# Attention scores of a head pair: two bursts of 64-row products become one, and score and projection banks are shared

## The chip, the cores and the metric

One Trainium2 chip, one of its cores. The number that counts is the device time of one launch in microseconds (us). The kernel before takes 2736.12 us, the median of three runs (2734.57 to 2736.74).

## The reference

For 32 sequences (batch index b) of 256 rows of width 256: a cross attention with 16 heads of width 64 over 512 keys (256 rows of a side tensor and 256 rows of a context tensor, each with weights of its own), a residual, then a small quantised layer, and a second residual.

```python
q = layernorm(x) @ Wq.T + bq                          # 16 heads of 64
k = concat(side @ Wk.T + bk, ctx @ Wgk.T + bgk)       # 512 keys
v = concat(side @ Wv.T + bv, ctx @ Wgv.T + bgv)
att = q @ k.T / 8;  att[..., :256] = where(mask, -inf, att[..., :256])
x = x + softmax(att) @ v @ Wo.T + bo
x = x + fp8_gemm(layernorm(x), kernel) + ffn_bias
```

## The kernel before

Everything is written in five instruction streams, one for each engine, in an order written out by hand for one batch. The streams run a first batch, a hardware loop over the next 30 and a last batch. The engines meet only through semaphores; no scheduler moves anything.

Per batch the stream of TensorE (PE) holds 89 calls of four kinds.

- `scores(c, h, t)`: the scores of one tile of 128 query rows for the head pair h, h+1. A head is 64 wide, so a product uses 64 of the array's 128 rows: the two heads of a pair lie in the two halves of the partitions, and their products start together. Numbers are split into a high and a low part, so three products are summed: k_hi by q_hi, k_hi by q_lo, k_lo by q_hi. A call is thus a burst of 3 steps of 2 products, 512 columns each. There are 16 such calls a batch: 8 pairs by 2 tiles. They write the PSUM tensor `ps_scores`, two banks, one for each head of the pair.
- `chunk(c, kind, n)`: a projection into one bank of `ps_misc` (two banks, taken in turn). Kinds k0, k1, v0, v1 and q are keys, values and queries of head group n (12 products of 128 rows and 256 columns each); wo0 and wo1 are the output projection of the batch before (16 matmul records each); xq, ff and zt are short.
- `transposes(c, h, k)`: four 128 by 128 transposes of the normalised probabilities of head h, into `ps_pt` (two banks).
- `outputs(c, h)`: probabilities times values, 8 products, into `ps_o` (two banks).

The other engines follow. VectorE (DVE) `mins` (L1144) adds the mask to a bank of scores, writes `probs` and takes the row minimum; ScalarE (ACT) `exps` (L875) takes exponentials; DVE `recip`, then GpSimd (POOL) `norm` (L477) scales; after the transposes ACT `pt_his` (L882) and DVE `pt_los` (L1155) split the result into high and low parts. `o_los` on ACT (L889) and `o_adds` on DVE (L1163) empty `ps_o`. Projections are emptied by `copy_keys` on ACT (L852), `split_his` on ACT (L840) with `split_los` on DVE (L1050), or `copy_values` on DVE (L1075); POOL splits keys and values once more.

What sets the order around the change: before a `scores` call PE waits on `min_done` until the minima of the two heads of the tile before have been taken (the one buffer of scores is empty). Before a `chunk` it waits on `misc_free` of that chunk's bank. `probs` is a ring of four heads: minima of head h wait for the transposes of the heads up to h-4, and for h+1 up to h-3.

Of the kernel before, what the change touches and what calls it, by code (L numbers as in the profile page):

```python
# [33 lines left out]
P = 128  # L34
# [49 lines left out]
MISC_BANKS = 2  # L84
KV_RING = 4
BANK = {chunk: i % MISC_BANKS for i, chunk in enumerate(CHUNKS)}
# [11 lines left out]
class Batch:  # L98
# [20 lines left out]
    def before(self, chunk, kinds, bank=None):  # L119
        return self.earlier(kinds, bank) + counted(self.chunks[:self.chunks.index(chunk)], kinds, bank)  # L120

# [23 lines left out]
def xattn_ffn_kernel(nc, x, side_t, ctx_t, mask, wq_t, bq, wk_t, bk, wgk_t, bgk, wv_t, bv, wgv_t, bgv,  # L145
                     wo_t, bo, ffn_w, s_in, s_k, ffn_bias, out):
    with ExitStack() as ctx:
# [89 lines left out]
        misc_full = [sem(f"misc_full{i}") for i in range(MISC_BANKS)]  # L237
        misc_free = [sem(f"misc_free{i}") for i in range(MISC_BANKS)]
# [12 lines left out]
        kvhi_done = sem("kvhi_done")  # L251
# [151 lines left out]
        def _(pool):  # L403
# [23 lines left out]
            def split_rows(c, part):  # L427
# [3 lines left out]
                if not (isinstance(c.b, int) and c.b < 0):  # L431
                    chunk = (("v0", 3), ("v1", 3))[part]
                    pool.wait_ge(misc_full[BANK[chunk]], c.through(chunk))
# [5 lines left out]
                nc.gpsimd.tensor_scalar(kv_hi[:, :, keys], raw, 1.0, 0.0, ALU.mult, ALU.add).then_inc(kvhi_done, 1)  # L439
                pool.wait_ge(kvhi_done, 2 * (n - 1) + part + 1)  # L440
# [19 lines left out]
            def kv_hi_of(c, kind, n):  # L460
                if (kind, n) in c.chunks:
                    src, hi, _ = kv_parts(kind, n)
                    wait_apart(pool, "pool", misc_free[BANK[kind, n]], c.through((kind, n)))
                    nc.gpsimd.tensor_scalar(hi, src, 1.0, 0.0, ALU.mult, ALU.add).then_inc(kv_hi_part, 1)  # L464
# [20 lines left out]
            def add_ffn_bias(c):  # L485
                if not c.first:
                    pool.wait_ge(misc_free[BANK["ff_prev", 0]], c.through(("ff_prev", 0)))
# [20 lines left out]
            def batch(c):  # L508
# [6 lines left out]
                kv_hi_of(c, "k1", 1)  # L515
                norm(c, 3, 0)
                norm(c, 3, 1)
                kv_lo_of(c, "k1", 1)
                rstd_of_y(c)
                copy_x(c)  # L520
                norm(c, 4, 0)
                norm(c, 4, 1)
                kv_hi_of(c, "v0", 1)
                norm(c, 5, 0)
                norm(c, 5, 1)
                scale_quant_in(c)
                kv_lo_of(c, "v0", 1)
# [5 lines left out]
                norm(c, 6, 0)  # L533
                norm(c, 6, 1)
                kv_lo_of(c, "v0", 2)
                norm(c, 7, 0)
                norm(c, 7, 1)
                kv_hi_of(c, "k1", 2)
                kv_lo_of(c, "k1", 2)
                kv_hi_of(c, "v1", 2)  # L540
                kv_lo_of(c, "v1", 2)
                norm(c, 8, 0)
                norm(c, 8, 1)
                norm(c, 9, 0)
                kv_hi_of(c, "k0", 3)
                norm(c, 9, 1)
                rstd_of_x(c)
# [3 lines left out]
                split_rows(c, 0)  # L551
                norm(c, 10, 0)
                norm(c, 10, 1)
                kv_hi_of(c, "v0", 3)
                norm(c, 11, 0)
                norm(c, 11, 1)
                split_rows(c, 1)
                kv_lo_of(c, "v0", 3)
                kv_hi_of(c, "v1", 3)
                norm(c, 12, 0)  # L560
                norm(c, 12, 1)
                norm(c, 13, 0)
                kv_lo_of(c, "v1", 3)
                kv_hi_of(c, "k0", 0)
                norm(c, 13, 1)
                kv_lo_of(c, "k0", 0)
                add_ffn_bias(c)
                norm(c, 14, 0)
                norm(c, 14, 1)
                kv_hi_of(c, "v0", 0)  # L570
                kv_lo_of(c, "v0", 0)
                finish(c)
                norm(c, 15, 0)
                norm(c, 15, 1)
                kv_hi_of(c, "k1", 0)
                kv_lo_of(c, "k1", 0)
                kv_hi_of(c, "v1", 0)
                norm(c, 16, 0)
                norm(c, 16, 1)
                kv_lo_of(c, "v1", 0)  # L580

# [12 lines left out]
        def _(pe):  # L594
# [11 lines left out]
            def chunk(c, kind, n):  # L606
                if (kind, n) not in c.chunks:
                    return
                if kind == "q" and n == 0:
                    pe.wait_ge(misc_free[BANK["zt_next", 0]], c.through(("zt_next", 0)))  # L610
# [8 lines left out]
                if kind == "ff_prev":  # L619
                    pe.wait_ge(misc_free[BANK["xq_prev", 0]], c.through(("xq_prev", 0)))  # L620
                bank = BANK[kind, n]
                if some(c.fills_before((kind, n))):
                    pe.wait_ge(misc_free[bank], c.fills_before((kind, n)))
                run_chunk(kind, n, bank).then_inc(misc_full[bank], 1)

            def run_chunk(kind, n, bank):

                halves = [ps_misc[:, bank, j * S:(j + 1) * S] for j in range(2)]
# [37 lines left out]
            def scores(c, h, t):  # L666
# [5 lines left out]
                if t == 0:  # L672
                    for ready in needed:
                        through = c.through if h >= H or n > 0 else c.through_last
                        if ready[0] == "q":
                            pe.wait_ge(misc_free[BANK[ready]], through(ready))
# [47 lines left out]
            scores(c, H, 0)  # L724
            scores(c, H, 1)
            pe.wait_ge(wo_loaded, 16)

            def batch(c):
                chunk(c, "k0", 1)
                scores(c, 2, 0)  # L730
                outputs(c, -1)
                transposes(c, 0, 0)
                transposes(c, 0, 1)
                scores(c, 2, 1)
                chunk(c, "q", 1)
                transposes(c, 1, 0)
                transposes(c, 1, 1)
                outputs(c, 0)
                chunk(c, "wo0_prev", 0)
                chunk(c, "k1", 1)  # L740
                transposes(c, 2, 0)
                transposes(c, 2, 1)
                scores(c, 4, 0)
                chunk(c, "wo1_prev", 0)
                scores(c, 4, 1)
                chunk(c, "q", 2)
                transposes(c, 3, 0)
                outputs(c, 1)
                scores(c, 6, 0)
                transposes(c, 3, 1)  # L750
                chunk(c, "v0", 1)
                chunk(c, "k0", 2)
# [630 lines left out]
```

## Time and profile before

| | |
|---|---|
| median of three runs | 2736.12 us |
| the profiled execution | 2734.6 us |
| span of its trace | 2732.8 us |
| PE busy | 2677.5 us, 98% |
| DVE busy | 2163.6 us, 79% |
| POOL busy | 2048.8 us, 75% |
| ACT busy | 1859.6 us, 68% |
| granted TensorE clock, mean | 0.995 |

The span lies between the first and the last instruction of the profiled execution; the execution's own time is 1.8 us longer. A start in the timeline is the moment a group of instructions begins; matmuls overlap, so the cost of a PE instruction is read from the distance between two starts, not from its duration. In the chain of work each piece lasts until the next one of the chain begins.

### The profile page before, as it was taken

The numbers are of one execution on the slowest core, as the hardware profiler recorded it, in microseconds if no ns is written. First come the engines' busy times: TensorE is split into PE (matmuls) and PEld (weight loads), VectorE is DVE, ScalarE is ACT, GpSimd is POOL, SyncE is SP. The second block draws the span as 40 slices with busy tenths as digits, with TensorE's granted clock in tenths as the row PEclk, the third lists the DMA queues.
The fourth block names the chain that finished last, engine by engine and source line by source line (L and its number), as shares of the span: only waits on it lengthen the run. The fifth ranks groups of instructions, "written<-read, shape, count | busy, mean of one in ns | idle before, by whom it ended". The sixth has DMA issues, their size and how long they took to land.

```text
span 2732.8 us, 66539 instructions
## 1 busy us (share of the span) xinstructions
PE 2677.5 (98%) x20352; PEld 2349.6 (86%) x20352; DVE 2163.6 (79%) x5329; ACT 1859.6 (68%) x4454; POOL 2048.8 (75%) x2503
## 2 busy tenths in 40 slices
PE   5999999999999999999999999999999999999996
PEld 4888888888888888888888888888888888888885
DVE  5888777888778887778877788887788877788875
ACT  4766667766667666677666676666776666776664
POOL 4787777877777877777877778777788777787774
PEclk9999999999999999999999999999999999999998
DMA  3000000001000000000000000000000100000100
GB/s 144 24 24 24 27 27 23 27 19 31 23 27 27 27 19 27 27 23 27 19 31 23 27 27 27 19 27 27 26 24 19 31 27 24 26 27 19 31 16 8
DMA packets 57246, 75.18 MB, mean 28 GB/s; under 512 B 4992, under 2 KB 39296, under 8 KB 57216
## 3 DMA queue, kind: packets, MB, share of 16 engines
q1 hardware_dynamic: 57216, 74.81, 9.0%
q8 instruction: 15, 0.25, 0.0%
q14 instruction: 15, 0.12, 0.0%
HBM read 66.40 MB, written 8.39 MB: 27 GB/s over the span
## 4 chain that ended last, share of the span: by engine, by line
PE 80%; ACT 7%; issue 6%; DVE 5%; DMA 0%; SPq 0%; POOL 0%; DVEq 0%; ACTq 0%; POOLq 0%
PE ps_misc L603 28%; PE ps_scores L685 15%; PE ps_o L712 15%; PE ps_pt L697 13%; PE ps_misc L653 8%; ACT probs L875 3%; DVE probs L1144 2%; ACT pt_hi L882 2%; DVE pt_lo L1155 2%; ACT kv_out L852 1%; DVE o_t L1163 1%; PE ps_misc L662 1%; PE ps_misc L632 0%; DMA probs<-wv_t_dram 0%; ACT q_hi L840 0%
## 5 line engine op out<-in xcount | busy, mean ns | idle before, releaser
L477 POOL TENSOR_SCALAR probs<-probs,recips 128x512 f32<-128x512 f32 x1024 | 729.7, 723 | 330.2 <-DVE recips L1151 324.2
L875 ACT ACTIVATE probs<-probs,neg_max 128x512 f32<-128x512 f32 x1024 | 739.7, 725 | 214.8 <-DVE neg_max L1144 205.4
L1144 DVE CUSTOM_DVE_ANT_1 probs<-ps_scores,mask_sb 128x512 f32<-128x512 f32 x960 | 636.2, 685 | 217.9 <-PE ps_scores L685 177.6
L882 ACT CAST pt_hi<-ps_pt 128x512 fp32r<-128x512 f32 x1024 | 565.6, 589 | 306.7 <-PE ps_pt L697 300.0
L1155 DVE TENSOR_TENSOR pt_lo<-ps_pt,pt_hi 128x512 fp32r<-128x512 f32 x1024 | 675.6, 683 | 108.1 <-ACT pt_hi L882 107.0
L697 PE MATMUL ps_pt<-ident,probs 128*128 128x128 f32 x4096 | 554.2, 274 | 6.1 <-POOL probs L477 3.7
L712 PE MATMUL ps_o<-pt_hi,v_hl 128*128 128x256 f32 x2048 | 548.6, 302 | 3.0 <-DVE pt_lo L1155 3.0
L712 PE MATMUL ps_o<-pt_lo,v_hl 128*128 128x256 f32 x2048 | 508.1, 282 | 0.0
L697 PEld LDWEIGHTS ps_pt<-ident,probs 128*128 128x128 f32 x4096 | 457.3, 141 | 46.8 <-issue 35.5
L712 PEld LDWEIGHTS ps_o<-pt_hi,v_hl 128*128 128x128 f32 x2048 | 387.0, 189 | 62.0 <-issue 58.0
L712 PEld LDWEIGHTS ps_o<-pt_lo,v_hl 128*128 128x128 f32 x2048 | 389.3, 190 | 0.0
L470 POOL TENSOR_TENSOR v_hl<-kv_out,v_hl 128x512 fp32r<-128x512 f32 x256 | 346.7, 1354 | 8.1
L470 POOL TENSOR_TENSOR k_lo<-kv_out,k_hi 128x512 fp32r<-128x512 f32 x256 | 331.5, 1295 | 13.4
L889 ACT COPY o_lo<-ps_o 64x256 f32<-64x256 f32 x512 | 189.6, 370 | 181.2 <-DVE o_t L1163 167.0
L464 POOL TENSOR_SCALAR k_hi<-kv_out 128x512 fp32r<-128x512 f32 x256 | 166.2, 649 | 169.3 <-ACT kv_out L852 169.3
L685 PE MATMUL ps_scores<-k_hi,q_hi 64*128 64x512 f32 x1024 | 256.2, 497 | 6.2 <-DVE neg_max L1144 3.2
L852 ACT ACTIVATE kv_out<-ps_misc,qk_bias 128x256 f32<-128x256 f32 x512 | 215.4, 475 | 57.7 <-PE ps_misc L603 55.3
L464 POOL TENSOR_SCALAR v_hl<-kv_out 128x512 fp32r<-128x512 f32 x256 | 175.5, 686 | 93.4 <-DVE kv_out L1075 93.4
L653 PE MATMUL ps_misc<-wo_sb,o_t 128*128 128x256 f32 x1024 | 237.7, 386 | 1.5 <-DVE o_t L1163 0.9
L653 PEld LDWEIGHTS ps_misc<-wo_sb,o_t 128*128 128x128 f32 x1024 | 191.6, 192 | 37.4 <-issue 12.2
L1163 DVE TENSOR_TENSOR o_t<-ps_o,o_lo 64x256 f32<-64x256 f32 x480 | 198.5, 414 | 27.2 <-ACT o_lo L889 20.2
L685 PE MATMUL ps_scores<-k_hi,q_lo 64*128 64x512 f32 x1024 | 203.3, 393 | 0.0
(105 smaller groups left out, 5846.1 us busy)
## 6 DMA issues: line engine op xcount, KB each, us to landing
mask_sb<-mask_dram SPq DMA_DIRECT2D x128, 256.0 KB, 3.1
x_sb<-x_dram SPq DMA_DIRECT2D x32, 256.0 KB, 2.7
side_raw<-side_t_dram SPq DMA_DIRECT2D x32, 256.0 KB, 3.8
scr_b<-ctx_t_dram SPq DMA_DIRECT2D x32, 256.0 KB, 2.7
out_dram<-y SPq DMA_DIRECT2D x32, 256.0 KB, 2.1
probs<-wq_t_dram SPq DMA_DIRECT2D x1, 1024.0 KB, 5.0
o_t<-wk_t_dram SPq DMA_DIRECT2D x1, 1024.0 KB, 7.3
wo_sb<-wgk_t_dram SPq DMA_DIRECT2D x1, 1024.0 KB, 9.3
```

Source lines behind the costliest of these rows:

```text
L464: nc.gpsimd.tensor_scalar(hi, src, 1.0, 0.0, ALU.mult, ALU.add).then_inc(kv_hi_part, 1)
L470: nc.gpsimd.tensor_tensor(lo, src, hi.bitcast(F32), ALU.subtract).then_inc(kv_ready, 1)
L477: nc.gpsimd.tensor_scalar(p, p, recips[:, h % RING, t:t + 1], 1.0, ALU.mult, ALU.mult).then_inc(norm_done, 1)
L603: last = mm(dst, a(t), c(t), start=(n == 1), stop=(n == 3 * DT))
L653: last = mm(dst, o_t[:, p, tile], wo_sb[:, p, :], start=(p == 0), stop=(p == H // 2 - 1))
L685: last = mm(ps_scores[:, e, :], q[own, n % 2, a, rows], k[own, n % 2, a, :], start=(i == 0), stop=(i == 2))
L697: last = nc.tensor.transpose(ps_pt[:, k, j, t * P:(t + 1) * P], probs[:, h % RING, t, kt * P:(kt + 1) * P], ident[:])
L712: last = mm(ps_o[:, h % 2, 0:S], v_hl[:, n % 2, kt, i, :], pt[:, h % 2, kt, :], start=(kt == 0 and pt is pt_hi), stop=(kt == KT - 1 and pt ...
L875: nc.scalar.activation(p, p, ACT.Exp, bias=neg_max[:, h % RING, t:t + 1], scale=-1.0, accum_out=sums[:, h % RING, t:t + 1]).then_inc(exp_d ...
L882: nc.scalar.copy(pt_hi[:, h % 2, 2 * k:2 * k + 2, :], ps_pt[:, k, :, :]).then_inc(pthi_done, 1)
L1144: V.tensor_tensor_reduce(out=p, in0=s, in1=mask_sb[:, row::MASK_ROWS - row, :], scale=MASK_STEP, scalar=SCORE_LIMIT, op0=ALU.add, op1=ALU.min,
L1155: V.tensor_tensor(pt_lo[:, h % 2, 2 * k:2 * k + 2, :], ps_pt[:, k, :, :], pt_hi[:, h % 2, 2 * k:2 * k + 2, :].bitcast(F32), ALU.subtract). ...
```

## The change

`ps_scores` and `ps_misc` become one tensor `ps_work` of four banks. `scores(c, h, 0)` writes banks 0 and 1 (one for each head of the pair), `scores(c, h, 1)` writes banks 2 and 3. The two calls now stand one behind the other for each of the eight pairs, so a burst has 6 steps of 2 products. The chunks use the same four banks, each by a table. A chunk therefore waits in addition (`after=(h, t)`) until DVE has taken the minima of the scores that lay in its bank, and a `scores` call waits until the chunks that used its two banks have been emptied (`after=` names the last of them for each bank). The work is the same, instruction for instruction; the orders of all four compute engines' streams are new. The list of chunks and the ring of `probs` stay.

```diff
+BANKS = 4
-BANK = {chunk: i % MISC_BANKS for i, chunk in enumerate(CHUNKS)}
+BANK = {
+    ("k0", 1): 0, ("q", 1): 1, ("wo0_prev", 0): 3, ("k1", 1): 2, ("wo1_prev", 0): 0,
...
-        ps_scores = psum("ps_scores", [P, 2, NK])
+        ps_work = psum("ps_work", [P, BANKS, 512])
         ps_pt = psum("ps_pt", [P, 2, 2, S])
         ps_o = psum("ps_o", [P, 2, 512])
-        ps_misc = psum("ps_misc", [P, MISC_BANKS, 512])
...
-            def chunk(c, kind, n):
+            def chunk(c, kind, n, after=None):
+
                 if (kind, n) not in c.chunks:
                     return
+                if after:
+                    h, t = after
+                    pe.wait_ge(min_done, 2 * (c.head(h) + t) + BANK[kind, n] % 2 + 1)
...
-                if some(c.head(h) + t):
-                    pe.wait_ge(min_done, 2 * (c.head(h) + t))
+                if some(c.head(h)):
+                    pe.wait_ge(min_done, 2 * (c.head(h) + t) - 2)
+                for e, chunk_before in enumerate(after):
+                    bank = 2 * t + e
+                    if some(c.so_far(chunk_before, bank)):
+                        pe.wait_ge(chunk_free[bank], c.so_far(chunk_before, bank))
...
-                        last = mm(ps_scores[:, e, :], q[own, n % 2, a, rows], k[own, n % 2, a, :],
+                        last = mm(ps_work[:, 2 * t + e, :], q[own, n % 2, a, rows], k[own, n % 2, a, :],
...
-                s = ps_scores[:, h % 2, :].rearrange("p (k s) -> p k s", s=S)
+                s = ps_work[:, 2 * t + h % 2, :].rearrange("p (k s) -> p k s", s=S)
```

The new order of PE for one batch, where the eight pairs stand (of what is left out, only the calls next to a burst are named in the prediction):

```diff
+                scores(c, 2, 0, after=(None, None))
+                scores(c, 2, 1, after=(None, None))
+                transposes(c, 0, 0)
+                transposes(c, 0, 1)
+                chunk(c, "k0", 1, after=(2, 0))
...
+                chunk(c, "k1", 1, after=(2, 1))
                 transposes(c, 2, 0)
+                scores(c, 4, 0, after=(("k0", 1), ("q", 1)))
+                scores(c, 4, 1, after=(("k1", 1), ("wo0_prev", 0)))
                 transposes(c, 2, 1)
+                chunk(c, "wo1_prev", 0, after=(4, 0))
...
+                chunk(c, "k0", 2, after=(4, 1))
+                scores(c, 6, 0, after=(("wo1_prev", 0), ("v0", 1)))
+                scores(c, 6, 1, after=(("k0", 2), ("q", 2)))
                 outputs(c, 2)
...
                 transposes(c, 5, 1)
+                scores(c, 8, 0, after=(("v1", 1), ("v0", 2)))
+                scores(c, 8, 1, after=(("k0", 2), ("k1", 2)))
                 outputs(c, 4)
...
+                chunk(c, "k1", 3, after=(8, 1))
+                scores(c, 10, 0, after=(("v1", 2), ("q", 3)))
+                scores(c, 10, 1, after=(("xq_prev", 0), ("k1", 3)))
+                outputs(c, 7)
...
                 transposes(c, 9, 1)
+                scores(c, 12, 0, after=(("v1", 2), ("q", 3)))
+                scores(c, 12, 1, after=(("v1", 3), ("v0", 3)))
+                transposes(c, 10, 0)
+                chunk(c, "zt_next", 0, after=(12, 0))
...
                 outputs(c, 10)
+                scores(c, 14, 0, after=(("zt_next", 0), ("ff_prev", 0)))
+                scores(c, 14, 1, after=(("q", 0), ("v0", 3)))
                 transposes(c, 12, 0)
...
                 outputs(c, 12)
+                scores(c, 16, 0, after=(("zt_next", 0), ("k0", 0)))
+                scores(c, 16, 1, after=(("k1", 0), ("v0", 0)))
                 transposes(c, 14, 0)
                 transposes(c, 14, 1)
+                chunk(c, "v1", 0, after=(16, 0))
```

PE before, at the second tile of the pair 6, 7: the end of the chunk v1 of group 1 (`ps_misc`), the burst (`ps_scores`), the beginning of the outputs of head 3 (`ps_o`). The burst of the first tile stands 45 rows earlier.

```order
L603 MATMUL ps_misc<-wgv_hi,kv_hi 128x256
L603 MATMUL ps_misc<-wgv_hi,kv_lo 128x256
L603 MATMUL ps_misc<-wgv_lo,kv_hi 128x256
L685 MATMUL ps_scores<-k_hi,q_hi 128x512 x2
L685 MATMUL ps_scores<-k_hi,q_lo 128x512 x2
L685 MATMUL ps_scores<-k_lo,q_hi 128x512 x2
L712 MATMUL ps_o<-pt_hi,v_hl 128x256
```

PE now, at the same pair: the end of the chunk k0 of group 2, both tiles' scores, the outputs of head 2.

```order
L614 MATMUL ps_work<-kv_hi,wgk_hi 128x256
L614 MATMUL ps_work<-kv_hi,wgk_lo 128x256
L614 MATMUL ps_work<-kv_lo,wgk_hi 128x256
L707 MATMUL ps_work<-k_hi,q_hi 128x512 x2
L707 MATMUL ps_work<-k_hi,q_lo 128x512 x2
L707 MATMUL ps_work<-k_lo,q_hi 128x512 x2
L707 MATMUL ps_work<-k_hi,q_hi 128x512 x2
L707 MATMUL ps_work<-k_hi,q_lo 128x512 x2
L707 MATMUL ps_work<-k_lo,q_hi 128x512 x2
L734 MATMUL ps_o<-pt_hi,v_hl 128x256
```

The two bursts have moved together, and the chunk ahead of them, k0 of group 2, lies in bank 2, which the second tile's scores need three steps later.

DVE before, from the minima of pair 4, 5: the minima of the first tile (each with a read of its accumulator, `neg_max`), the low parts of head 2's transposes, then the minima of the second tile with an addition between them.

```order
L1144 ISA probs,neg_max<-ps_scores,mask_sb 128x512
L1144 ISA neg_max 128x1
L1144 ISA probs,neg_max<-ps_scores,mask_sb 128x512
L1144 ISA neg_max 128x1
L1155 TENSOR_TENSOR pt_lo<-ps_pt,pt_hi 128x512 x2
L1144 ISA probs,neg_max<-ps_scores,mask_sb 128x512
L1144 ISA neg_max 128x1
L1163 TENSOR_TENSOR o_first<-ps_o,o_lo 64x256
L1144 ISA probs,neg_max<-ps_scores,mask_sb 128x512
L1144 ISA neg_max 128x1
```

DVE now, at the same pair.

```order
L1166 ISA probs,neg_max<-ps_work,mask_sb 128x512
L1166 ISA neg_max 128x1
L1166 ISA probs,neg_max<-ps_work,mask_sb 128x512
L1166 ISA neg_max 128x1
L1166 ISA probs,neg_max<-ps_work,mask_sb 128x512
L1166 ISA neg_max 128x1
L1177 TENSOR_TENSOR pt_lo<-ps_pt,pt_hi 128x512
L1166 ISA probs,neg_max<-ps_work,mask_sb 128x512
L1166 ISA neg_max 128x1
```

The four minima of a pair now follow each other almost directly; the low parts of the transposes come between or behind them.

## Rows read from the trace of the kernel before

**Rows 1.** The page: span, busy time by engine.

```profile
span 2732.8 us, 66539 instructions
PE 2677.5 (98%) x20352; PEld 2349.6 (86%) x20352; DVE 2163.6 (79%) x5329; ACT 1859.6 (68%) x4454; POOL 2048.8 (75%) x2503
```

**Rows 2.** Two stretches: length, busy PE, PEld, DVE, ACT, POOL, then PEclk, DMA.

```profile
50.00:133.00 83.00, 79.08 (x609) 69.00 (x610) 67.04 (x164) 58.29 (x142) 61.00 (x74) 1.00 0.08 24
1200.00:1283.00 83.00, 82.93 (x636) 72.88 (x635) 67.08 (x166) 57.45 (x140) 63.50 (x79) 1.00 0.09 25
```

**Rows 3.** Timeline of PE, one row in each of two batches: start, us, instruction.

```profile
1180.55 0.60 PE L632 MATMUL ps_misc<-ident,scr_a 128*128 128x128 f32 x4
1263.89 0.60 PE L632 MATMUL ps_misc<-ident,scr_a 128*128 128x128 f32 x4
```

**Rows 4.** PE's waits over the whole span: total us, times, longest us.

```profile
PE ps_misc L603 <- DVE wv_lo L1184: 8.9, 1, 8.9
PE ps_scores L685 <- DVE neg_max L1144: 3.2, 2, 1.7
```

**Rows 5.** Timeline of PE around one burst.

```profile
1206.28 0.28 PE L603 MATMUL ps_misc<-kv_lo,wgk_hi 128*128 128x256 f32 x1
1206.49 0.49 PE L685 MATMUL ps_scores<-k_hi,q_hi 64*128 64x512 f32 x2
1206.83 0.39 PE L685 MATMUL ps_scores<-k_hi,q_lo 64*128 64x512 f32 x2
1207.06 0.40 PE L685 MATMUL ps_scores<-k_lo,q_hi 64*128 64x512 f32 x2
1207.40 0.38 PE L712 MATMUL ps_o<-pt_hi,v_hl 128*128 128x256 f32 x1
1207.62 0.29 PE L712 MATMUL ps_o<-pt_lo,v_hl 128*128 128x256 f32 x1
```

**Rows 6.** The chain of work inside one batch: start, us until the next piece.

```profile
1212.90 0.95 PE ps_o L712 x8
...
1226.65 0.44 PE ps_pt L697 x4
...
1228.04 0.89 PE ps_scores L685 x6
1228.93 0.59 PE ps_pt L697 x4
1229.52 2.85 PE ps_misc L603 x24
...
1235.70 1.15 PE ps_o L712 x8
```

**Rows 7.** Timeline of PE before the loop: two bursts with nothing between.

```profile
37.81 0.40 PE L685 MATMUL ps_scores<-k_lo,q_hi 64*128 64x512 f32 x2
39.88 0.50 PE L685 MATMUL ps_scores<-k_hi,q_hi 64*128 64x512 f32 x2 [1.68 <-DVE neg_max L1144]
40.21 0.39 PE L685 MATMUL ps_scores<-k_hi,q_lo 64*128 64x512 f32 x2
```

**Rows 8.** Timeline, all engines: a chunk's last product and its emptying.

```profile
1211.74 0.28 PE L603 MATMUL ps_misc<-zt_lo,wq_hi 128*128 128x256 f32 x1
...
1212.06 0.84 ACT L840 ACTIVATE q_hi<-ps_misc,qk_bias 128x256 fp32r<-128x256 f32 x2 [0.31 <-PE ps_misc L603]
```

**Rows 9.** Timeline of ACT and of DVE: a copy of keys, one minimum.

```profile
1201.09 0.85 ACT L852 ACTIVATE kv_out<-ps_misc,qk_bias 128x256 f32<-128x256 f32 x2
...
1207.84 0.69 DVE L1144 CUSTOM_DVE_ANT_1 probs<-ps_scores,mask_sb 128x512 f32<-128x512 f32 x1 [0.25 <-issue]
1208.46 0.08 DVE L1144 DVE_READ_ACCUMULATOR2_ANT neg_max<- 128x1 f32 x1
```

**Rows 10.** DVE's longest kind of wait: total us, times, longest us.

```profile
DVE probs L1144 <- PE ps_scores L685: 177.6, 193, 2.9
```

More of the change, by code:

```diff
@@ L120, in before, with so_far @@
         return self.earlier(kinds, bank) + counted(self.chunks[:self.chunks.index(chunk)], kinds, bank)
+    def so_far(self, chunk, bank):
+        upto = CHUNKS[:CHUNKS.index(chunk) + 1] if chunk else []
+        return self.earlier(ALL_KINDS, bank) + counted([c for c in self.chunks if c in upto], ALL_KINDS, bank)
     def fills_before(self, chunk):
@@ L664, in run_chunk, with scores @@
                 return last
-            def scores(c, h, t):
+            def scores(c, h, t, after):
                 if not c.has_head(h):
@@ L758, in batch @@
                 transposes(c, 4, 1)
-                chunk(c, "v0", 2)
-                chunk(c, "k1", 2)
+                chunk(c, "v1", 1, after=(6, 0))
+                chunk(c, "v0", 2, after=(6, 0))
+                chunk(c, "k1", 2, after=(6, 1))
                 transposes(c, 5, 0)
-                scores(c, 8, 0)
                 transposes(c, 5, 1)
+                scores(c, 8, 0, after=(("v1", 1), ("v0", 2)))
+                scores(c, 8, 1, after=(("k0", 2), ("k1", 2)))
                 outputs(c, 4)
-                chunk(c, "v1", 2)
@@ L766, in batch @@
-                scores(c, 8, 1)
+                outputs(c, 5)
                 transposes(c, 6, 0)
                 transposes(c, 6, 1)
-                chunk(c, "q", 3)
-                chunk(c, "k0", 3)
+                chunk(c, "v1", 2, after=(8, 0))
+                chunk(c, "q", 3, after=(8, 0))
                 transposes(c, 7, 0)
-                outputs(c, 5)
+                chunk(c, "k0", 3, after=(8, 1))
                 transposes(c, 7, 1)
                 outputs(c, 6)
-                scores(c, 10, 0)
@@ L776, in batch @@
-                chunk(c, "xq_prev", 0)
-                chunk(c, "k1", 3)
+                chunk(c, "xq_prev", 0, after=(8, 1))
+                chunk(c, "k1", 3, after=(8, 1))
+                scores(c, 10, 0, after=(("v1", 2), ("q", 3)))
+                scores(c, 10, 1, after=(("xq_prev", 0), ("k1", 3)))
+                outputs(c, 7)
                 transposes(c, 8, 0)
                 transposes(c, 8, 1)
-                outputs(c, 7)
-                scores(c, 10, 1)
-                chunk(c, "v0", 3)
@@ L789, in batch @@
-                chunk(c, "ff_prev", 0)
-                transposes(c, 10, 0)
                 transposes(c, 10, 1)
                 outputs(c, 9)
-                scores(c, 12, 1)
-                chunk(c, "q", 0)
+                chunk(c, "ff_prev", 0, after=(12, 0))
+                chunk(c, "q", 0, after=(12, 1))
                 transposes(c, 11, 0)
                 transposes(c, 11, 1)
-                scores(c, 14, 0)
                 outputs(c, 10)
-                chunk(c, "k0", 0)
+                scores(c, 14, 0, after=(("zt_next", 0), ("ff_prev", 0)))
@@ L802, in batch @@
                 outputs(c, 11)
-                scores(c, 14, 1)
-                chunk(c, "v0", 0)
+                chunk(c, "k0", 0, after=(14, 0))
+                chunk(c, "v0", 0, after=(14, 1))
+                chunk(c, "k1", 0, after=(14, 1))
                 transposes(c, 13, 0)
@@ L834, in split_his @@
                 bank = BANK[kind, n]
-                act.wait_ge(misc_full[bank], c.through((kind, n)))
+                act.wait_ge(chunk_full[bank], c.through((kind, n)))
                 for cols, hi, _, bias in split_parts(kind, n):
                     if bias is None:
-                        last = nc.scalar.copy(hi, ps_misc[:, bank, cols])
+                        last = nc.scalar.copy(hi, ps_work[:, bank, cols])
                     else:
-                        last = nc.scalar.activation(hi, ps_misc[:, bank, cols], ACT.Identity, bias=bias)
+                        last = nc.scalar.activation(hi, ps_work[:, bank, cols], ACT.Identity, bias=bias)
                 last.then_inc(hi_done, 1)
@@ L851, in copy_keys @@
                     half = slice(j * S, (j + 1) * S)
-                    last = nc.scalar.activation(kv_out[:, KV_TURN[kind, n], half], ps_misc[:, bank, half],
+                    last = nc.scalar.activation(kv_out[:, KV_TURN[kind, n], half], ps_work[:, bank, half],
                                                 ACT.Identity, bias=qk_bias[:, 1 + j, p:p + 1])
-                last.then_inc(misc_free[bank], 1)
+                last.then_inc(chunk_free[bank], 1)
             def copy_quantised(c):
@@ L1045, in split_los @@
                 for cols, hi, lo, bias in split_parts(kind, n):
-                    src = ps_misc[:, bank, cols]
+                    src = ps_work[:, bank, cols]
                     if bias is None:
@@ L1051, in split_los @@
                                                       op0=ALU.add, op1=ALU.subtract)
-                last.then_inc(misc_free[bank], 1)
+                last.then_inc(chunk_free[bank], 1)
             def moments(which, src, bn_ready, mv_ready, n):
```

341 lines of the change are left out of this document (163 added, 178 removed), and 4 rows, old and new, of the table BANK.

## The prediction, written before the changed kernel ran

> **What bounds the kernel now.** I read the busy shares first: PE is busy for 98% of the span, DVE, the next, for 79% [rows 1]. A share can hide a stage that is bound otherwise, so the table by stretches came next. In a stretch of 83 us in the middle of the loop PE idles for 0.07 us and its clock is granted in full; the stretch that begins at 50 us shows 79.08 us of 83, so the first batch alone waits [rows 2]. The same row begins in two neighbouring batches 83.34 us apart [rows 3]; 32 batches of that are 2667 us of the 2732.8, and the rest is the start and the end. In the waits of PE the longest is 8.9 us and happens once, in the preparation of the weights; for the banks of scores PE waited twice, 3.2 us together [rows 4]. So in the loop PE runs from instruction to instruction, and time can only come from the distances between its starts, or be lost by a wait that is not there now.
>
> **What a burst costs.** Plain products of 256 columns start 0.12 us apart: two chunks in a row, 24 products, are a piece of 2.85 us in the chain of work [rows 6]. Around one burst [rows 5], from the last plain product before it (1206.28) to the second one behind it (1207.62), it is 1.34 us, of which two plain distances are 0.24: the burst costs 1.10 us. Inside it the distances are 0.34 and 0.23, and 0.34 from the third step to the first product behind. The first plain product behind takes 0.22 to the next in place of 0.12. The chain of work says the same: the piece of a burst is 0.89 us, and the outputs behind a burst are a piece of 1.15 where those behind a transpose are 0.95. Transposes behind a burst cost a little less, 0.59 for 0.44 [rows 6].
>
> Put directly behind the first, the second tile's three steps should cost the inner distance, 0.23 each: one merged burst is 1.10 + 0.69 = 1.79 us where two single ones are 2.20. That is 0.41 us for each pair. Eight pairs make 3.3 us a batch. Before, three of sixteen bursts are followed by transposes, after it is five of eight; at 0.05 us each this is 0.1 us more. Against that, starts are rounded to 0.01 us, which counts three times in each pair, and one of the sixteen bursts today is followed by the short 16-bit transposes of the quantised rows, which may lose less. I choose 0.39 us for a pair, at the lower side, **3.1 us a batch**; 3.3 stays as the upper end.
>
> The trace before has one place with two bursts and nothing between, ahead of the loop, and there PE had waited 1.68 us for minima. Behind that wait the first inner distance is 0.33 again, with no other mode in between [rows 7]. The long first step belongs to a start after a pause as well, and the seam in a merged burst costs between nothing and 0.10 us. I take nothing where its waits have been met in time: the 24 products of rows 6 are two chunks, each with a wait at its head, and their mean distance stays at 0.119.
>
> The Trainium skill (TensorEngine Tiling (Array Packing), Tiling Modes, Key Properties) says that a change of the tiling mode drains the engine, and not a change of tile in one mode. By the rule alone the seam is free and the gain 3.1 us; by rows 7, which show a long first step without a change of mode, it would be 3.1 - 8 x 0.10 = 2.3.
>
> **What the new waits cost.** Counts of instructions on DVE, ACT and POOL do not change, nor do the DMAs that SP issues or what they wait for (minima, which are all done in the same number). Four cases:
>
> *The second tile waits for a chunk directly ahead.* At two pairs a keys' chunk stands right before the burst and lies in a bank of the second tile: k0 of group 2 before pair 6 (bank 2), k1 of group 3 before pair 10 (bank 3). From the chunk's last product to the second tile's first it is 0.21 + 0.34 + 0.23 + 0.23 = 1.01 us [rows 5]. To empty a bank takes longer: a chunk's last product starts at 1211.74, ACT begins at 1212.06 and needs 0.84, so it is free at 1212.90, 1.16 us later [rows 8]; the keys' copy takes 0.85 [rows 9]. With the way back to PE I put 0.2 to 0.25 us on each, if ACT is idle at that moment, which its order allows (it holds only the copy of the transposes issued before the chunk). Two places: 0.45 us. In pair 4 the chunk k1 of group 1 is one group of four transposes (0.44 us) further off and just makes it: 1.45 against 1.16.
>
> *A chunk waits for the minima in its bank.* A minimum occupies DVE for 0.62 us and its read 0.08 [rows 9]. The near places are pairs 2, 4, 12 and 16, where the first chunk in bank 0 comes 0.4 to 0.9 us (one or two groups of transposes) behind the second tile's 0.8. So 1.2 to 1.7 us lie between the start of the gap (the first tile's last step, which runs 0.40 us on) and the chunk; the minimum with its start needs 0.40 + 0.1 + 0.7 = 1.2. It fits only if DVE stands ready. At pair 2 it does: the work in front, the addition of head 14's output, is issued before the burst. At pair 12 the low part of a transpose stands in front, at pair 16 one too, but both groups of transposes were issued before the burst. I put 0.05 us on these four together and keep 1 us each as the other end, below.
>
> *The probabilities.* Between a pair's burst and the transposes of its first head PE now has at least 6.8 us of other work (pair 16: the two groups of transposes of head 14, v1, outputs 13, transposes 15, outputs 14, then the next burst, 0.87 + 1.5 + 0.95 + 0.87 + 0.95 + 1.6). From the first minimum to the scaled row the work is four minima (2.5 us), an exponential (0.9) and two scalings on POOL (1.4), some 5.5 us with the waits. Covered with about 1.3 us to spare.
>
> *DVE as a whole.* It is busy 67.1 us of 83 now [rows 2]; of 80.7 that is 83%. Still behind PE, but its slack shrinks from 16 to 14 us a batch.
>
> **The sum.** 83.3 - 3.1 + 0.5 = 80.7 us a batch, 2.6 us less. The first batch waits for other things, so I count 31: 81 us. The profiled execution took 2734.6, which gives 2654. The median of the runs is 1.5 us above it, so 2655.
>
> **Rivals.**
>
> A, *the seam is not free*. Each of the eight seams pays the 0.10 us of rows 7 because the second tile's waits, up to three of them, stop the products of its first step from being prepared. Then the gain is 2.6 - 0.8 = 1.8 us, times 31 is 56: 2680. For it: the only two adjacent bursts in the trace. Against it: there PE stood still in between.
>
> B, *slower: DVE comes late to the banks*. Today DVE waits for scores 193 times, 177.6 us in all [rows 10]: the scores are what comes late, not DVE. After the change 4 banks fill in 1.7 us and DVE needs 2.5 us to empty them. If at the near places (pairs 2, 4, 12, 16) it first has to finish one low part that itself waits for ACT's copy (0.6 + 0.6 us), and then the second pair of minima is late for the next chunk too, PE stands for 1 us each; the other four pairs, with one 0.3 us stall each, bring it to 5.2. Less the 3.1 that is 2.1 us a batch, 65 us in all: 2801. It decides from 0.39 us lost at each pair on. Against it: in front of each of these minima, in the order of DVE, stands work whose input PE has issued before the burst. The Trainium skill (TensorEngine Tiling, PSUM Bottleneck) warns of this: tiling speeds up TensorE, not the emptying of PSUM. No row here shows a bank that is late.
>
> C, *the gain is eaten but not more*: the second tile waits at most pairs, so that bursts stay split in fact. A split burst costs 0.39 and the wait by itself 0.1 to 0.2. At half the pairs that leaves 3.1 - 4 x 0.55 = 0.9 us, 28 us in all: 2708; at all of them nothing is left.
>
> **Chances.** My forecast 0.66, A 0.14, C 0.09 (of it 0.02 within 0.2% of no change), B 0.09, the full 3.3 us with no stall (31 x 3.3 = 102: 2634) 0.02. Range 2634 to 2705: from the full gain to C with half the pairs split. A difference of 0.2% (5.5 us) is about what a measurement of this kernel can tell. Faster 0.89, same 0.02, slower 0.09.
>
> **What would show it.** In the timeline after: the two tiles of a pair start their steps 0.23 us apart across the seam (0.33 speaks for A); the same row of two neighbouring batches lies 80.7 us apart; the waits of PE show the second tile waiting for ACT's copy of keys twice a batch, 0.2 us each, some 62 times. B would show as PE in chunks waiting for DVE's minima, for more than 100 us over the span. I am wrong if PE's idle time in a stretch of one batch is above 1 us, or the inner steps grow when two tiles stand together.

## The result, and the profile after

The changed kernel takes 2662.5 us (median of four runs, 2660.8 to 2664.3) against 2735.7 for the kernel before (four runs): a ratio of 0.973, with a 95% interval of 0.972 to 0.975. The forecast was 2655, with 2634 to 2705 as its range. The profiled execution took 2661.8 us, 72.8 less than the 2734.6 of before; 81 were forecast.

The page of the kernel after, and its table of one stretch of 81 us (length, busy PE, PEld, DVE, ACT, POOL with counts, PEclk, DMA), answer to [rows 1, 2]:

```profile
span 2660.0 us, 67352 instructions
PE 2595.8 (98%) x20352; PEld 2352.2 (88%) x20352; DVE 2122.6 (80%) x5329; ACT 1846.9 (69%) x4454; POOL 2045.4 (77%) x2503
```

```profile
1200.00:1281.00 81.00, 80.58 (x637) 73.07 (x636) 65.75 (x166) 57.14 (x140) 63.73 (x78) 1.00 0.09 26
```

The same row in two neighbouring batches, as in [rows 3], from the timeline of PE after:

```profile
1233.72 0.63 PE L647 MATMUL ps_work<-ident,scr_a 128*128 128x128 f32 x4
...
1314.94 0.63 PE L647 MATMUL ps_work<-ident,scr_a 128*128 128x128 f32 x4
```

They lie 81.22 us apart, where it was 83.34. PE is still what bounds the loop, now with 0.42 us of idle time in 81, at the same clock. Cut at that row, the 30 full periods of the loop carry 62.9 us of the 72.8, what lies before them 0.8, and what lies behind them, the last batch with the tail, 9.1.

The merged burst, where nothing is late (pair 8, timeline of PE after; it answers to [rows 5]):

```profile
1211.48 0.50 PE L707 MATMUL ps_work<-k_hi,q_hi 64*128 64x512 f32 x2
1211.81 0.39 PE L707 MATMUL ps_work<-k_hi,q_lo 64*128 64x512 f32 x2
1212.05 0.39 PE L707 MATMUL ps_work<-k_lo,q_hi 64*128 64x512 f32 x2
1212.28 0.39 PE L707 MATMUL ps_work<-k_hi,q_hi 64*128 64x512 f32 x2
1212.51 0.40 PE L707 MATMUL ps_work<-k_hi,q_lo 64*128 64x512 f32 x2
1212.73 0.40 PE L707 MATMUL ps_work<-k_lo,q_hi 64*128 64x512 f32 x2
1213.06 0.39 PE L734 MATMUL ps_o<-pt_hi,v_hl 128*128 128x256 f32 x1
```

The distances are 0.33, 0.24, 0.23, 0.23, 0.22, and 0.33 to the product behind. Across the seam, the step from the first tile's last products to the second tile's first (1212.05 to 1212.28), it is 0.23, as inside a burst.

The burst of pair 6, where the chunk k0 of group 2 stands directly ahead (timeline of PE after; the ACT row is from the timeline of ACT):

```profile
1201.04 0.28 PE L614 MATMUL ps_work<-kv_lo,wgk_hi 128*128 128x256 f32 x1
1201.25 0.50 PE L707 MATMUL ps_work<-k_hi,q_hi 64*128 64x512 f32 x2
...
1201.81 0.40 PE L707 MATMUL ps_work<-k_lo,q_hi 64*128 64x512 f32 x2
1202.43 0.50 PE L707 MATMUL ps_work<-k_hi,q_hi 64*128 64x512 f32 x2 [0.22 <-ACT kv_out L874]
1202.76 0.40 PE L707 MATMUL ps_work<-k_hi,q_lo 64*128 64x512 f32 x2
```

```profile
1201.36 0.84 ACT L874 ACTIVATE kv_out<-ps_work,qk_bias 128x256 f32<-128x256 f32 x2 [0.79 <-PE ps_work L614]
```

The seam is 0.62 us in place of 0.23, and the first distance behind it 0.33 in place of 0.23. ACT ends at 1202.20, and PE starts 0.23 us after that. Pair 10 has a seam of 0.51 (median of the batches, as for all medians below). Its rows, PE and then ACT:

```profile
1223.65 0.28 PE L614 MATMUL ps_work<-kv_lo,wgk_hi 128*128 128x256 f32 x1
...
1224.42 0.40 PE L707 MATMUL ps_work<-k_lo,q_hi 64*128 64x512 f32 x2
1224.94 0.51 PE L707 MATMUL ps_work<-k_hi,q_hi 64*128 64x512 f32 x2
```

```profile
1224.05 0.84 ACT L874 ACTIVATE kv_out<-ps_work,qk_bias 128x256 f32<-128x256 f32 x2 [0.97 <-PE ps_work L614]
```

The parts of the delay differ here: ACT begins 0.40 us behind the chunk's last product (0.32 in pair 6), and PE follows ACT's end, 1224.89, by 0.05 us (0.23 in pair 6). The third place is behind the burst of pair 2: eight transposes, then k0 of group 1, which must have the minimum of the first head. PE first, then DVE:

```profile
1177.17 1.09 PE L719 MATMUL ps_pt<-ident,probs 128*128 128x128 f32 x8
1178.34 0.39 PE L614 MATMUL ps_work<-kv_hi,wk_hi 128*128 128x256 f32 x1
```

```profile
1176.26 0.69 DVE L1177 TENSOR_TENSOR pt_lo<-ps_pt,pt_hi 128x512 fp32r<-128x512 f32 x1
...
1176.87 0.41 DVE L1185 TENSOR_TENSOR o_t<-ps_o,o_lo 64x256 f32<-64x256 f32 x1
1177.59 0.69 DVE L1166 CUSTOM_DVE_ANT_1 probs<-ps_work,mask_sb 128x512 f32<-128x512 f32 x1 [0.32 <-PE ps_work L707]
1178.21 0.08 DVE L1166 DVE_READ_ACCUMULATOR2_ANT neg_max<- 128x1 f32 x1
```

The transposes' starts take 0.87 (8 of 0.109) and end in a chunk at once elsewhere; here the chunk starts 1.17 behind the first of them, 0.3 late. The minimum is read at 1178.21 to 1178.29, and PE starts at 1178.34. The first tile's scores had been ready since about 1176.6; DVE still had a low part and an addition of the old batch to do until 1177.28, and then stood for 0.32 us at the beginning of its next batch.

PE's waits over the whole span, after (total, times, longest), answer to [rows 4]:

```profile
PE ps_work L707 <- ACT kv_out L874: 6.6, 30, 0.2
...
PE ps_work L614 <- DVE neg_max L1166: 2.1, 1, 2.1
```

This list shows 0.2 us for 30 of some 60 late seams and none of the 30 late chunks. The reason is in the durations: a product counts as busy for 0.40 us while the next could start after 0.23, so the first part of each pause is no idle time. What is left of it, 0.22 us in pair 6, 0.12 in pair 10 and 0.08 at the chunk of pair 2, makes the 0.42 of the stretch, and the list has only the first of the three. The distances of the starts show the whole. So, in part, does the same list for PE's weight loads (PEld), which overlap less:

```profile
PEld ps_work L707 <- ACT kv_out L874: 16.6, 30, 0.6
PEld ps_work L614 <- DVE neg_max L1166: 11.8, 31, 2.3
```

That is 0.55 us for each of 30 late seams, pair 10's (pair 6's stand under `issue`), and 0.3 for each of the 30 late chunks (the 31st, of 2.3, is outside the loop). Loads also stand idle where nothing is late (0.36 us ahead of an output behind a burst), so their idle time is a place to look and not yet a cost.

### The profile page after: what moved, and what is told of

It is laid out like the page before. It is cut to its first block, busy times and chain, and to the rows that moved or that the text cites. A ratio compares the mean times of both kernels' runs of the same rounds, so it can differ in the third digit from the quotient of the medians.

```text
span 2660.0 us, 67352 instructions
## 1 busy us (share of the span) xinstructions
PE 2595.8 (98%) x20352; PEld 2352.2 (88%) x20352; DVE 2122.6 (80%) x5329; ACT 1846.9 (69%) x4454; POOL 2045.4 (77%) x2503
## 4 chain that ended last, share of the span: by engine, by line
PE 91%; DVE 3%; ACT 3%; issue 2%; DMA 0%; SPq 0%; POOL 0%; DVEq 0%; POOLq 0%; ACTq 0%
PE ps_work L614 35%; PE ps_o L734 18%; PE ps_pt L719 16%; PE ps_work L707 13%; PE ps_work L668 8%; ACT pt_hi L904 1%; DVE o_t L1185 1%; ACT kv_out L874 1%; DVE pt_lo L1177 1%; PE ps_work L647 1%; DVE probs L1166 1%; PE ps_work L677 1%; DMA probs<-wv_t_dram 0%; ACT o_lo L911 0%; PE ps_work L673 0%
## 5 line engine op out<-in xcount | busy, mean ns | idle before, releaser
L488 POOL TENSOR_SCALAR probs<-probs,recips 128x512 f32<-128x512 f32 x1024 | 711.7, 708 | 247.7 <-DVE recips L1173 247.6
L1166 DVE CUSTOM_DVE_ANT_1 probs<-ps_work,mask_sb 128x512 f32<-128x512 f32 x960 | 619.7, 685 | 125.2 <-PE ps_work L707 123.1
L734 PE MATMUL ps_o<-pt_hi,v_hl 128*128 128x256 f32 x2048 | 535.3, 296 | 1.4 <-DVE pt_lo L1177 1.4
L874 ACT ACTIVATE kv_out<-ps_work,qk_bias 128x256 f32<-128x256 f32 x512 | 216.2, 477 | 196.5 <-PE ps_work L614 196.5
L707 PE MATMUL ps_work<-k_hi,q_hi 64*128 64x512 f32 x1024 | 236.9, 459 | 14.6 <-ACT kv_out L874 6.6
L668 PE MATMUL ps_work<-wo_sb,o_t 128*128 128x256 f32 x1024 | 231.6, 379 | 0.9 <-DVE o_t L1185 0.9
L475 POOL TENSOR_SCALAR v_hl<-kv_out 128x512 fp32r<-128x512 f32 x256 | 183.5, 717 | 54.2 <-DVE kv_out L1097 54.2
L668 PEld LDWEIGHTS ps_work<-wo_sb,o_t 128*128 128x128 f32 x1024 | 189.6, 190 | 24.3 <-DVE o_t L1185 1.1
L707 PE MATMUL ps_work<-k_hi,q_lo 64*128 64x512 f32 x1024 | 202.5, 391 | 0.0
```

The source lines that it names most:

```text
L488: nc.gpsimd.tensor_scalar(p, p, recips[:, h % RING, t:t + 1], 1.0, ALU.mult, ALU.mult).then_inc(norm_done, 1)
L668: last = mm(dst, o_t[:, p, tile], wo_sb[:, p, :], start=(p == 0), stop=(p == H // 2 - 1))
L707: last = mm(ps_work[:, 2 * t + e, :], q[own, n % 2, a, rows], k[own, n % 2, a, :], start=(i == 0), stop=(i == 2))
L734: last = mm(ps_o[:, h % 2, 0:S], v_hl[:, n % 2, kt, i, :], pt[:, h % 2, kt, :], start=(kt == 0 and pt is pt_hi), stop=(kt == KT - 1 and pt ...
L1166: V.tensor_tensor_reduce(out=p, in0=s, in1=mask_sb[:, row::MASK_ROWS - row, :], scale=MASK_STEP, scalar=SCORE_LIMIT, op0=ALU.add, op1=ALU.min,
```

## The experiments

All were made from the changed kernel, unless said otherwise, and are compared with its 2662.5 us. Each ran beside runs of the kernel before (2733.2 to 2734.4 us median), which sets an uncertainty of some 1 to 2 us between kernels of different groups.

**All eight bursts split.** The second tile one group later:

```diff
                 scores(c, 8, 0, after=(("v1", 1), ("v0", 2)))
-                scores(c, 8, 1, after=(("k0", 2), ("k1", 2)))
                 outputs(c, 4)
+                scores(c, 8, 1, after=(("k0", 2), ("k1", 2)))
```

> The changed kernel, with one edit: in all eight pairs the second tile's scores stand one group later in PE's stream (behind one group of four transposes in pairs 2, 4, 12, 14, 16, behind one head's outputs in pairs 6, 8, 10). Banks, waits and the other engines' orders stay. My theory (the merged burst is what gains, by saving one entry and one exit of 64-row products for each pair): each split gives back 0.28 us where transposes stand between and 0.39 us where outputs do, 2.6 us a batch; against it the two late second tiles (0.48 and 0.38 us a batch) and part of the late chunk of pair 2 (0.33) are covered again. Net +1.4 to +1.7 us in 31 batches: 2705 to 2716 us. Rival (the four shared banks and the new orders gain, not the merging): within 5 us of the changed kernel, 2662.

Measured: 2749.5 us, 0.54% slower than the kernel before (ratio 1.005, 1.004 to 1.007), and 87 above the merged one. The period is 83.83. The splits themselves cost 0.39 us each where outputs stand between, as expected, and 0.30 where transposes do, counted up to the end of the second tile; in four of the five pairs what follows that tile takes longer as well (a second group of transposes by 0.05 us), so a split costs 0.35 there (medians of the distances). Together they are some 2.9 us a batch. The late seams went. But new waits came that I had not expected: 0.77 us behind the transposes of head 8, for the minima of pair 10, and 0.2 behind the first tile of pair 12. The first is in its list of waits and in its timeline:

```profile
PE ps_work L614 <- DVE neg_max L1166: 19.2, 33, 2.2
```

```profile
1182.24 0.50 PE L707 MATMUL ps_work<-k_hi,q_hi 64*128 64x512 f32 x2
...
1183.14 1.09 PE L719 MATMUL ps_pt<-ident,probs 128*128 128x128 f32 x8
1184.76 0.38 PE L614 MATMUL ps_work<-wv_hi,kv_hi 128*128 128x256 f32 x1 [0.53 <-DVE neg_max L1166]
```

The second tile comes at 1182.24, only eight transposes later stands the chunk v0, and its bank holds scores that DVE has not yet read. So the banks and the new orders without the merging gain nothing here, and the rival that they were the source of the 73 us has fallen. How far they lose belongs to this order, which was made for merged bursts: without the two new waits the period would be about 82.9, a little under the 83.33 of before. No run tried the shared banks with an order made for split bursts.

**Four bursts split**, in pairs 8, 12, 14 and 16, where nothing had been late.

> As the split of all pairs, but only in pairs 8, 12, 14 and 16, where the changed kernel waits for nothing. My theory: one split behind outputs (0.39) and three behind transposes (0.28 each in the distances of starts of the trace before) are +1.2 us a batch, 37 us in 31 batches: 2699. Rival (orders and banks gain): 2662. Rival (the seam costs as much as a split, only waits count): 2662 too.

Measured: 2710.7 us (ratio to the kernel before 0.992, 0.990 to 0.993), 48 more than the merged one where 37 were expected; both rivals of "no change" fall. Its timeline in pair 14:

```profile
1180.69 0.50 PE L707 MATMUL ps_work<-k_hi,q_hi 64*128 64x512 f32 x2
1181.02 0.39 PE L707 MATMUL ps_work<-k_hi,q_lo 64*128 64x512 f32 x2
1181.26 0.39 PE L707 MATMUL ps_work<-k_lo,q_hi 64*128 64x512 f32 x2
1181.58 0.66 PE L719 MATMUL ps_pt<-ident,probs 128*128 128x128 f32 x4
1182.17 0.50 PE L707 MATMUL ps_work<-k_hi,q_hi 64*128 64x512 f32 x2
```

From the third step to the next tile it is 0.91 us. Merged it is 0.23, and the four transposes take 0.44 of their own; the 0.24 that are left are most of what the split costs. The period rose by 1.53 us: 0.39 + 3 x 0.30 = 1.29 for the splits, 0.15 for a wait in pair 12 as above, and 0.1 for the transposes behind the second tile in pairs 14 and 16 (0.41 in place of 0.36 us each).

**Two outputs moved to cover the keys' copies.**

```diff
+                outputs(c, 2)
                 scores(c, 6, 0, after=(("wo1_prev", 0), ("v0", 1)))
                 scores(c, 6, 1, after=(("k0", 2), ("q", 2)))
-                outputs(c, 2)
...
-                outputs(c, 6)
                 chunk(c, "xq_prev", 0, after=(8, 1))
                 chunk(c, "k1", 3, after=(8, 1))
+                outputs(c, 6)
                 scores(c, 10, 0, after=(("v1", 2), ("q", 3)))
```

> The changed kernel with the outputs of head 2 moved from behind the scores of pair 6 to ahead of them, and the outputs of head 6 from ahead of the chunks xq and k1 of group 3 to ahead of the scores of pair 10, so that 0.95 us of products stands between a keys' chunk and the second tile that needs its bank. My theory: the two late seams (0.61 and 0.51 us in place of 0.23, then 0.33 in place of 0.23) go, 0.86 us a batch, 27 us: 2635. Rival (the wait only moves, since ACT or DVE sets the pace there): less than a third of it, 2655 to 2662.

Measured: 2689.0 us (0.984, 0.982 to 0.985): 27 slower, not 27 faster. Both late seams went as expected (0.23). Three other waits took their place:

```profile
PE ps_work L614 <- ACT kv_out L874: 21.7, 32, 1.0
PE ps_o L734 <- DVE pt_lo L1177: 9.7, 33, 1.3
```

```profile
1149.45 0.39 PE L673 MATMUL ps_work<-ident_bf,xq 128*128 128x128 bf16 x4
1150.50 0.39 PE L614 MATMUL ps_work<-kv_hi,wk_hi 128*128 128x256 f32 x1 [0.66 <-ACT kv_out L874]
```

k1 of group 3 lies in bank 3 like k0 of group 3 two groups earlier; head 6's outputs had covered the emptying between them, and my edit took the cover away (0.84 us). And PE waited 0.42 us in the outputs of head 5 and 0.31 us behind the transposes of head 8. The expectation failed on what the moved group had hidden.

**Only head 2's outputs moved**, the first half of that edit.

> The changed kernel with only the outputs of head 2 moved ahead of the scores of pair 6. In the run in which head 6's outputs moved too, the late seams had gone, but PE waited 0.42 us in outputs 5, 0.31 us behind the transposes of head 8, and 0.84 us for k1 of group 3, whose bank 3 still held k0 of group 3. Theory: the wait in outputs 5 belongs to this edit, because the burst of pair 6 and with it its minima come 0.95 us later; the other two belong to head 6's edit. Then this one gains 0.48 and loses 0.42: 2659 to 2663. Rival (the wait in outputs 5 belongs to head 6's edit or to both): 0.48 us a batch faster, 2647.

Measured: 2663.9 us (0.974, 0.973 to 0.976), in the range of the theory. The wait is there, in the outputs of head 5, and in the distances it is 0.46 us against the 0.48 gained:

```profile
1134.05 0.39 PE L734 MATMUL ps_o<-pt_hi,v_hl 128*128 128x256 f32 x1 [0.30 <-DVE pt_lo L1177]
```

A burst moved back by one group moves its minima, and with them all that follows on DVE up to the low part that the next outputs wait for. That the low part is late for this reason and no other is argued from the order; the run shows only that it belongs to this edit.

**A third late seam made on purpose.**

```diff
-                chunk(c, "k1", 2, after=(6, 1))
                 transposes(c, 5, 0)
                 transposes(c, 5, 1)
+                chunk(c, "k1", 2, after=(6, 1))
                 scores(c, 8, 0, after=(("v1", 1), ("v0", 2)))
```

> The changed kernel with the chunk k1 of group 2 (bank 3) moved behind the transposes of head 5, so that it stands directly ahead of the scores of pair 8; ACT's copy of it moves behind its copies of head 5's transposes. My theory (a keys' chunk directly ahead of the burst makes the second tile late, and a missed wait costs the pause and a long first step of 0.33): a third late seam like the two there are, 0.51 to 0.61 us in place of 0.23 and 0.10 more behind it, 0.38 to 0.48 us a batch, 12 to 15 us: 2674 to 2677. Rival (the seams of pairs 6 and 10 are late by something peculiar to them): 2662.

Measured: 2674.8 us (0.978, 0.977 to 0.980), 12.3 more, in the range of the theory. Its timeline in pair 8:

```profile
1135.14 0.40 PE L707 MATMUL ps_work<-k_lo,q_hi 64*128 64x512 f32 x2
1135.58 0.51 PE L707 MATMUL ps_work<-k_hi,q_hi 64*128 64x512 f32 x2
1135.92 0.40 PE L707 MATMUL ps_work<-k_hi,q_lo 64*128 64x512 f32 x2
```

A seam of 0.44 and then 0.34, where it was 0.23 and 0.23. The seam is shorter than the 0.51 to 0.61 expected, and the period rose by 0.35 us, a little under the 0.38 to 0.48 of the theory; the total is in its range because some 2 us came outside the loop. So at all three places the second tile is late right behind a keys' chunk, and a missed wait costs the long first step on top, with nothing shown as idle in the row.

**Head 15's outputs ahead of k0 of group 1.**

```diff
+                outputs(c, -1)
                 chunk(c, "k0", 1, after=(2, 0))
                 chunk(c, "q", 1, after=(2, 0))
-                outputs(c, -1)
```

> The changed kernel with the outputs of head 15 of the batch before moved ahead of the chunk k0 of group 1, the first chunk behind the scores of pair 2, which waits 0.3 us for the minimum in its bank. My theory: DVE is late there by its work left from the end of the batch and by the turn of its loop; 0.95 us of products covers it, 0.33 us a batch, 10 us: 2652. Rival (DVE is late for the whole stretch, so that a later wait takes the place): 2660 to 2662.

Measured: 2651.4 us (0.970, 0.969 to 0.971), 11 faster, as the theory had it. Apart from the groups exchanged, none took more than 0.06 us longer or shorter than in the changed kernel, so DVE was late at one place, not for a stretch.

**On top of it, k0 of group 2 ahead of four transposes.**

```diff
                 transposes(c, 3, 0)
-                transposes(c, 3, 1)
                 chunk(c, "k0", 2, after=(4, 1))
+                transposes(c, 3, 1)
```

> On top of the kernel with head 15's outputs moved (2651): the chunk k0 of group 2 goes ahead of the second transposes of head 3, ACT's copy of it likewise. The burst of pair 6 keeps its place, and 0.53 us of transposes stand between the chunk and the burst. Theory: the late seam of pair 6 nearly goes (0.26 as in pair 4, where the same distance stands), 0.45 us a batch, 14 us: 2637, if nothing else becomes late. Rival (the minima of pair 6, now behind a later low part of head 3 on DVE, are late for what follows, as when the burst itself was moved): 2648 to 2655.

Measured: 2638.3 us (0.965, 0.964 to 0.966), 13 faster than the last, as the theory had it. The seam of pair 6 is 0.23, with 0.28 behind it, and no other wait took its place: the burst had stayed where it was.

**On top of that, pair 10.**

```diff
-    ("k1", 2): 3, ("v1", 2): 0, ("q", 3): 1, ("k0", 3): 3, ("xq_prev", 0): 2,
-    ("k1", 3): 3, ("v0", 3): 3, ("v1", 3): 2, ("zt_next", 0): 0, ("ff_prev", 0): 1,
+    ("k1", 2): 3, ("v1", 2): 0, ("q", 3): 1, ("k0", 3): 3, ("xq_prev", 0): 3,
+    ("k1", 3): 2, ("v0", 3): 3, ("v1", 3): 2, ("zt_next", 0): 0, ("ff_prev", 0): 1,
...
-                outputs(c, 6)
-                chunk(c, "xq_prev", 0, after=(8, 1))
                 chunk(c, "k1", 3, after=(8, 1))
+                chunk(c, "xq_prev", 0, after=(8, 1))
+                outputs(c, 6)
```

> As the last one, and for pair 10: k1 of group 3 in bank 2 and xq in bank 3, in the order transposes 7, k1, xq, outputs 6, scores of pair 10, so that neither chunk waits for k0 of group 3 and 0.95 us of products stand ahead of the burst. Theory: the seam of pair 10 goes too, 0.38 us a batch, 12 us more: 2625. Rival: the burst keeps its place, so I know of none but xq coming late from DVE (0.3 us or more): 2634.

Measured: 2634.5 us (0.964, 0.963 to 0.965), 4 faster, not 12. The seam of pair 10 is 0.23, but behind the transposes of head 8 PE now waits 0.31 us, as in the run with two outputs moved: with the seam closed, it comes 0.38 us earlier to the chunk v0 of group 3, which needs the pair's fourth minimum. The late seam had hidden that.

**And v0 and v1 of group 3 with their banks exchanged.**

```diff
-    ("k1", 3): 2, ("v0", 3): 3, ("v1", 3): 2, ("zt_next", 0): 0, ("ff_prev", 0): 1,
+    ("k1", 3): 2, ("v0", 3): 2, ("v1", 3): 3, ("zt_next", 0): 0, ("ff_prev", 0): 1,
```

> On top of the last kernel (2634.5): the banks of v0 and v1 of group 3 change places, so that v0, the first chunk behind the scores of pair 10, lies in bank 2, whose minimum DVE takes 0.62 us before that of bank 3. In the last kernel PE waited 0.31 us a batch behind the transposes of head 8 for the minimum in bank 3. Theory (that wait is for the fourth minimum of pair 10): it goes, 0.3 us a batch, 9 us: 2625. Rival (the wait is for the emptying of an earlier chunk, or the next wait takes its place): 2632 to 2635.

Measured: 2624.9 us (ratio to the kernel before 0.960, 0.958 to 0.961), 10 faster, as the theory had it; 37.6 us or 1.4% faster than the changed kernel. This is the version that beats both. Its stretch of 81 us, columns as above:

```profile
1200.00:1281.00 81.00, 81.00 (x647) 74.45 (x646) 66.33 (x169) 58.15 (x142) 64.67 (x80) 1.00 0.09 26
```

PE does not idle at all there, and the period is 79.95 us. In the distances nothing is late by more than 0.06 us.

## Why the prediction was right, and where a size was off

*PE bounds the loop, and the distances between its starts are the price.* Right. In the split runs each burst more costs 0.30 to 0.39 us, and the new waits account for the rest of the change in period.

*The merged burst saves 0.39 us, 3.1 a batch.* Right, and a little low. In the last kernel, which has the same merged bursts and hardly a wait left, the period is 79.95, so merging and the removal of the old waits are worth 83.33 - 79.95 = 3.38 us. The sum by the rows had come to 3.3, and I had chosen 3.1 and kept what PE waited in the loop before, which the stretch of 0.07 us idle did not let me see: the second tile of pair 10 started 0.35 us behind the last product of the outputs ahead of it, where the others take 0.21, so some 0.14 us of the 3.38 is an old wait. These runs show the price of going from one kind of product to the other and back. That the 64 rows make it, and not the 512 columns, is not isolated; between 128 and 256 columns on full rows nothing is lost on balance (four transposes ahead of a chunk take 0.35 in place of 0.44 us, and the chunk 1.51 in place of 1.42).

*The seam is free where its waits are met.* Right: 0.23 us. The six seams that were not late show 0.23, and the step behind them 0.23 to 0.26, so rival A did not happen there. Its long first step came at the two late ones, 0.33 behind the pause. So the rule of the Trainium skill (TensorEngine Tiling (Array Packing), Tiling Modes, Key Properties), that only a change of the tiling mode drains, agrees with the seams; and the long first step of [rows 7] belongs to a start after a pause, which these traces show without any change of mode.

*The waits cost 0.5 us a batch.* This is the term that was mis-sized: 1.24 us. The two late seams were placed right, but cost 0.48 and 0.38 in place of 0.2 to 0.25 each. In both, 0.10 is the long first step after the pause, which [rows 7] had shown and which I priced only for rival A. The rest of the excess is in pair 6 that PE starts 0.23 us after ACT's end, for which I had allowed under 0.1, and in pair 10 that ACT begins 0.40 us behind the chunk in place of 0.32. At the four near places I had put 0.05 us together, and had written of pair 2 that DVE stands ready there. It does not: 0.33 us. What I had left out is the end of DVE's own batch and 0.32 us at its turn into the next. Pairs 12 and 16 were met in time, and pair 4 lost 0.03 in the step behind its seam.

*31 batches of the difference.* The loop gave less, 30 x 2.1 = 63 us, and the last batch with the tail 9 us, which I had counted as 2.6. There the span is one of waits between engines. From the row of the last full period to its last product PE idles 14.3 us after and 17.5 before: inside the last batch seven pauses of 0.4 to 2.1 us became three of 0.3, 2.4 and 1.4. The other 6 us are less busy time, and I have not traced them.

*How near the forecast came.* In part this is luck. The waits cost some 22 us more in 30 batches than forecast, and against them stand 8 us more from the merged bursts and 7 more from the start and the end. The forecast range also stops at 2705, just under the 2708 that its own case C gives.

*Rival B, DVE late at the banks.* Not here, with one place of 0.33 us. But with the bursts split it came at once (0.77 and 0.2 us a batch), and made that version slower than the kernel before. So banks can be late for DVE's minima here, and in the merged order they are late at one place only.

*What I had named as a sign of error*, idle time above 1 us in a stretch of a batch, would have misled: it was 0.42 while 1.24 us were lost.

## What to carry to other kernels

Count the changes between products on half and on the full array in the stream of a bound TensorE, and put the half-array groups together: here a merged pair saved about 0.4 us against the order before, and 0.30 to 0.39 against split ones. When their results fill every free bank at once, let no chunk that shares a bank stand directly ahead of the burst or directly behind it, and look which groups hid a wait before they are moved. Where instructions overlap, as PE's do here, read waits from the distances of the starts, since pauses shorter than the overlap appear as busy; the idle time of the weight loads tells where to look.

## What the runs showed of the hardware

- A missed semaphore wait on PE costs more than its length: the first distance behind the pause is 0.33 to 0.34 us in place of 0.23 (pairs 6 and 10, and pair 8 in the third late seam).
- From the end of ACT's copy to the start of the products that waited for it, 0.23 us passed in pair 6 and 0.05 in pair 10 and in pair 8 of the third late seam, in all 30 batches of the loop; from the end of DVE's accumulator read to the chunk of pair 2 it was 0.05. The waits' order fits this. In pair 6 the late bank is bank 2, the first of the two chunks' banks that the tile waits for: the trace has this wait of PE's sequencer passed at 1202.23, a register step behind it, and the weight load, which carries the wait for bank 3, at 1202.42. In pairs 10 and 8 the late bank is bank 3, the last wait, and nothing is left to do behind it. No run exchanged the two waits alone.
- DVE stood 0.31 us (0.32 in the rows above) between the last addition of one batch and the first minimum of the next, in nearly every turn of the loop, with the scores long ready. The records of DVE's sequencer fill it: the loop's register and branch steps run from 0.85 to 0.40 us ahead of the minimum, most of it beside the addition, and behind them come two waits that are met at once, 0.35 and 0.15 us ahead of it. So it is the sequencer's time and no wait for another engine; how much of it an order without the turn would save was not tried.
